# Causal mask of two attentions moved from TensorE to VectorE, with reordered stage heads and earlier row gathers, in a six-stage decoder

## What is computed

```
x += attention(ln(x))            # 16 heads of 32, causal softmax                     "a0"
x += cross(ln(x), ctx, mask)     # softmax over 1024 masked context rows              "m"
x += experts(ln(x))              # 16 routed, 6 per token, sigmoid gate, 2 shared     "f0"
x += grouped_attention(ln(x))    # 32 heads of 64, 8 groups, rms norm, rotary, causal "a1"
x += linear_attention(ln(x), ctx)                                                   # "lin"
x += experts(ln(x))              # 8 routed, 2 per token, 1 shared                    "f1"
```

## Time and profile before

| what | value |
|---|---|
| median of 3 runs | 2163.74 us (2163.08 to 2165.18) |
| the profiled execution itself | 2166.24 us |
| span of its trace | 2165.0 us |
| mean granted TensorE clock in it | 0.941 of full speed |
| busy: TensorE, VectorE, GpSimd, ScalarE | 88%, 52%, 44%, 36% of the span |

### The profile page before, as it was taken

One profiled execution on the slowest core, in us unless ns is written; L12 is line 12 of the kernel. 1 busy time (PEld: TensorE's weight loads), 2 busy tenths in 40 slices (PEclk: granted clock), 3 DMA queues, 4 the chain that ended last, 5 costly groups with the idle time before them and its releaser, 6 DMA issues. The chain is left out here.

```text
span 2165.0 us, 31041 instructions
## 1 busy us (share of the span) xinstructions
PE 1910.6 (88%) x10658; PEld 1625.4 (75%) x10658; DVE 1134.7 (52%) x2385; ACT 780.4 (36%) x2029; POOL 961.7 (44%) x922
## 2 busy tenths in 40 slices
PE   5888978878999999899569999999997899898895
PEld 3776756657899889798447888888876688785784
DVE  4555675446333333235746666666665646456344
ACT  2555543231222222121136555655553323212231
POOL 2332242158872858704636445454442100106584
PEclk7999999999999999899779999999999899799998
DMA  2444432035653546322433233232320210003465
GB/s 83 137 120 124 153 125 78 1 108 199 213 202 119 179 151 219 135 73 88 151 78 98 78 85 103 61 86 77 80 59 26 78 44 1 20 1 101 175 213 172
DMA packets 102630, 232.36 MB, mean 107 GB/s; under 512 B 18752, under 2 KB 19008, under 8 KB 99408
## 3 DMA queue, kind: packets, MB, share of 16 engines
q1 hardware_dynamic: 82736, 144.89, 21.9%
q0 software_dynamic: 19744, 85.47, 11.6%
HBM read 126.23 MB, written 57.93 MB: 85 GB/s over the span
## 5 line engine op out<-in xcount | busy, mean ns | idle before, releaser
L615 POOL TENSOR_SCALAR a_E<-a_E,a_inv 128x128 f32<-128x128 f32 (+3 forms) x384 | 219.3, 589 | 287.4 <-DVE a_inv L734 287.4
L140 PE MATMUL bank<-f_UH,f_XH 128*128 x596 | 203.0, 341 | 19.8 <-POOL f_UL L152 14.8
L729 DVE TENSOR_REDUCE a_top<-bank 128x1 f32<-128x512 f32 (+3 forms) x384 | 164.1, 483 | 83.8 <-PE bank L881 81.3
L649 ACT ACTIVATE a_E<-bank,a_top 128x512 f32<-128x512 f32 (+3 forms) x384 | 199.0, 553 | 9.8 <-DVE a_top L729 9.8
L640 ACT ACTIVATE a_PHL<-bank 128x512 fp32r<-128x512 f32 (+1 forms) x288 | 131.0, 527 | 186.0 <-PE bank L897 185.8
L140 PE MATMUL bank<-f_UH,f_XL 128*128 x596 | 195.3, 328 | 0.0
L140 PE MATMUL bank<-f_UL,f_XH 128*128 x596 | 195.3, 328 | 0.0
L140 PE MATMUL bank<-a_PHL,a_VH 128*128 128x512 f32 (+3 forms) x768 | 181.7, 325 | 0.3 <-DVE a_QL L152 0.3
L152 DVE TENSOR_TENSOR a_PHL<-bank,a_PHL 128x512 fp32r<-128x512 f32 (+1 forms) x288 | 154.4, 590 | 27.3 <-ACT a_PHL L640 26.6
L1569 DVE TENSOR_TENSOR f_gate<-bank,f_gate 128x352 f32<-128x352 f32 x79 | 41.4, 524 | 216.4 <-PE bank L140 216.4
L1515 ACT ACTIVATE f_HH<-bank 128x256 fp32r<-128x256 f32 x220 | 60.0, 325 | 253.5 <-PE bank L1905 253.4
(11 more groups left out here) (384 smaller groups left out, 5130.1 us busy)
## 6 DMA issues: line engine op xcount, KB each, us to landing
f_uraw<-f_up POOLq DMA_DIRECT2D x18, 1408.0 KB, 6.3
f_xb<-table SPq DMA_DIRECT2D x86, 256.0 KB, 2.9
table<-f_ob SPq DMA_DIRECT2D x86, 256.0 KB, 2.1
table<-a_zeros SPq DMA_DIRECT2D x31, 512.0 KB, 4.2
f_draw<-f_down POOLq DMA_DIRECT2D x27, 512.0 KB, 4.2
a_g<-a_f SPq DMA_DIRECT2D x160, 64.0 KB, 2.0
a_raw<-a_qkv SPq DMA_DIRECT2D x36, 256.0 KB, 3.0
f_uraw<-f_up POOLq DMA_DIRECT2D x9, 704.0 KB, 4.8
```

The lines of the kernel that those rows point to most:

```text
L140: m = pe.matmul(out, a, b, start=first and i == 0 and j == 0, stop=last and i == n - 1 and j == 2, skip_group_check=not check)
L615: e.tensor_scalar(self.E[sl][:, a], self.E[sl][:, a], self.inv[:, sl, i:i + 1], 0.0, ALU.mult, ALU.add).then_inc(*self.s_nrm.up(N, m - 1, i))
L649: x = e.activation(self.E[sl][:, self.E_AT[i]:self.E_AT[i] + w], bank[:, off:off + w], ACT.Exp, bias=self.top[:, sl, i:i + 1], accum_out=s ...
L729: e.tensor_reduce(self.top[:, sl, i:i + 1], bank[:, off:off + P * (i + 1)], AX.X, ALU.max, negate=True).then_inc(*self.s_mx.up(N, m, i))
```

## The change

Three edits are made together.

1. *Mask*. The mask matmul goes, and so does the 128 x 128 tile; a 128 x 512 bf16 tile `causal` (zeros, and the triangle in its last 128 columns) is made by GpSimd in each attention. VectorE's maximum becomes one `tensor_tensor_reduce` per row block, which adds mask and scores, negates, writes the result to `E` in SBUF and gives the minimum. ScalarE's exponential reads and writes `E`. The bank is released by VectorE (`s_mx`) and no longer by ScalarE (`s_ex`).
2. *Heads*. m: the first batch's context is loaded by SP in round 20 of a0 and split while the norm's statistics run; on GpSimd the mask work comes after the context's low parts. lin: VectorE begins with the norm; all low parts of the key weights are GpSimd's; the context is loaded right after the key weights and split between norm tiles; its low parts come before those of the value weights. f0, f1: ScalarE's split of the first weights is cut in pieces, each behind a norm tile.
3. *Rows*. The gathers of odd `j` get their own buffers (the idle weight buffers and a few more). Those of `j = 1` are issued as soon as the tiles that can hold such rows are done, ahead of the end of the experts; a gather `j` waits for the add `j-2` and not for `j-1`.

```diff
@@ Attention.pool
+        e.memset(self.causal[:, :], 0.0).then_inc(*self.k.g.up())
         for z in (self.VH, self.VL):
...
+        last = self.causal[:, T - P:T]
+        e.affine_select(out=last, in_=last, compare_op=ALU.is_ge, fill=MASKED, base=0, pattern=[[-1, P]],
+                        channel_multiplier=1).then_inc(*self.s_zero.up(N))
@@ Attention.act
-                        x = e.activation(self.E[sl][:, self.E_AT[i]:self.E_AT[i] + w], bank[:, off:off + w], ACT.Exp,
-                                         bias=self.top[:, sl, i:i + 1], accum_out=self.total[:, sl, i:i + 1])
+                        E = self.E[sl][:, self.E_AT[i]:self.E_AT[i] + P * (i + 1)]
+                        x = e.activation(E, E, ACT.Exp, scale=-1.0, bias=self.top[:, sl, i:i + 1],
+                                         accum_out=self.total[:, sl, i:i + 1])
@@ Attention.dve
+        e.wait_ge(*self.s_zero.after(N))
...
-                        e.tensor_reduce(self.top[:, sl, i:i + 1], bank[:, off:off + P * (i + 1)], AX.X, ALU.max,
-                                        negate=True).then_inc(*self.s_mx.up(N, m, i))
+                        w = P * (i + 1)
+                        e.tensor_tensor_reduce(self.E[sl][:, self.E_AT[i]:self.E_AT[i] + w], self.causal[:, T - w:T],
+                                               bank[:, off:off + w], -1.0, HUGE, ALU.add, ALU.min,
+                                               self.top[:, sl, i:i + 1]).then_inc(*self.s_mx.up(N, m, i))
@@ Attention._pe_scores
-                t = e.matmul(bank[:, off + i * P:off + w], self.k.identb[:, :], self.k.causal[:, :],
-                             start=False, stop=True)
             t.then_inc(*self.s_s.up(N, m, ci))
-            emptied[bk] = self.s_ex.after(N, m, ci)
+            emptied[bk] = self.s_mx.after(N, m, chunk[-1][0])
@@ Attention.sp (a0, round m)
+                if m == 20:
+                    self.k.fetch_context()
@@ Memory.pool
-        self._masks(0)
         self._context_low(e, 0, range(KD), self.s_clo_pool)
+        self._masks(0)
@@ Mixture.pool
-                self._gather_early()
+                self._gather_early(0)
+            if w == W - 1 and self.shared > 1:
+                self._gather_early(1)
         if self.shared == 1:
-            e.wait_ge(*self.s_ev.after(N, "landed", self.OB - 1))
+            self._gather_early(1)
...
-        for j in range(1, self.top):
+        for j in range(2, self.top):
             for i in range(NT):
-                e.wait_ge(*self.s_x.after(N, j - 1, i))
+                e.wait_ge(*self.s_x.after(N, j - 2, i))
                 self._gather(j, i)
@@ Mixture._gather_early(j)
+        if j:
+            e.wait_ge(*self.s_ulo.after(N, W - 1))
+            e.wait_ge(*self.s_dlo.after(N, W - 1))
-        e.reg_load([reg], self.ends[0:1, self.R:self.R + 1])
+        e.reg_load([reg], self.ends[0:1, self.R + j:self.R + j + 1])
         e.wait_ge(self.s_ev.sem, reg)
@@ Mixture.act
-        self.norm.act(self._act_first, lambda i: self._act_logits(0) if i == TT else None)
+        self.norm.act(then=self._act_first)
@@ Mixture._act_first(i), behind norm tile i
+        if i < KD:                  # one of four pieces of UH
+        if i == TT:
+            self._act_logits(0)
+        if KD <= i < KD + 2:        # one of two pieces of DH
@@ Linear.sp
         self._load("k")
+        self._load_context(0, 0)
@@ Linear.pool
+        self._weights_low(e, "k", self.s_wlo_pool)
         for x in "kq":
...
-        self._weights_low(e, "k", self.s_wlo_pool)
@@ Linear.act
-        e.wait_ge(*self.s_fr.after())
-        for x in "kq":
-            e.activation(self.F[x][0][:, :], self.FR[x][:, :], ACT.Copy).then_inc(*self.s_fhi.up(x))
         self._weights_high("k")
-        self.norm.act()
+        self.norm.act(then=self._act_first)   # F behind tiles 0 and 1, the context behind tiles 2 to 5
@@ Linear.dve
-        self._weights_low(e, "k", self.s_wlo_dve)
         self.norm.dve()
+        self._context_low(e, 0, 0, (0, 2), self.s_clo_dve)
```

More of the change, by code:

```diff
@@ L1185, in _pe_scores @@
                     [(self.CH[:, kk, a], self.CL[:, kk, a]) for kk in range(KD)], last=False)
+            if i % TT == 0 and h == 0:
+                e.wait_ge(*self.s_mb.after(b))
             e.matmul(self.k.bank[bk][:, :], self.ones[:, :], self.mb[:, b, a], start=False, stop=True).then_inc(
@@ L1220, in __init__ @@
         self.rows = [sb(f"row{i}", [D])[:, :] for i in range(NT)]
+        raw = self.uraw[:, :, :].rearrange("p k n -> p (k n)")
+        spare = [raw[:, a:a + D] for a in range(0, KD * cols - D + 1, D)] + [self.draw[:, c, :] for c in range(3)]
+        self.back = [self.rows, spare + [sb(f"back{i}", [D])[:, :] for i in range(len(spare), NT)]]
         xb, ob = sb("xb", [self.XB * D]), sb("ob", [self.OB * D])
@@ L1287, in plan @@
         self.s_sent = [sig(f"sent{j}") for j in range(6)]
-        self.s_got = [sig(f"got{i}") for i in range(NT)]
+        self.s_got = [[sig(f"got{x}_{i}") for i in range(NT)] for x in range(2)]
         self.s_passed = sig("passed")
@@ L1315, in plan @@
             self.s_down.plan((N, w), 32)
-        for w in range(self.UB + 1, len(self.experts) + 1):
+        W = len(self.experts)
+        for w in range(self.UB + 1, W + 1):
             self.s_passed.plan((N, w))
-            if w == min(self.R - self.top + 4, len(self.experts)):
-                self.s_passed.plan((N, "early"))
+            if w == min(self.R - self.top + 4, W):
+                self.s_passed.plan((N, "early", 0))
+            if w == (W - 1 if self.shared > 1 else W):
+                self.s_passed.plan((N, "early", 1))
         for j in range(self.top):
@@ L1412, in pool @@
             if w == min(self.R - self.top + 4, W):
-                self._gather_early()
+                for j in range(self.top):
+                    e.wait_ge(*self.s_sent[j].after(N))
+                self._gather_early(0)
+            if w == W - 1 and self.shared > 1:
+                self._gather_early(1)
         if self.shared == 1:
-            e.wait_ge(*self.s_ev.after(N, "landed", self.OB - 1))
+            self._gather_early(1)
         else:
@@ L1624, in _add @@
         e, N, X = self.k.dve, self.name, self.k.X
-        e.wait_ge(*self.s_got[i].after(N, j))
+        e.wait_ge(*self.s_got[j % 2][i].after(N, j))
         e.wait_ge(*self.x_last[i])
-        e.scalar_tensor_tensor(out=X[:, i, :], in0=self.rows[i], scalar=self.wj[:, j, i:i + 1], in1=X[:, i, :],
+        e.scalar_tensor_tensor(out=X[:, i, :], in0=self.back[j % 2][i], scalar=self.wj[:, j, i:i + 1], in1=X[:, i, :],
                                op0=ALU.mult, op1=ALU.add).then_inc(*self.s_x.up(N, j, i))
@@ L1860, in _tables @@
         x = R - self.top
[L1861 removed]
+        e.tensor_scalar(self.ends[0:1, R:R + 2], end[0:1, x:x + 2], float(self.s_ev.value[N, NT - 1] + self.OB), None,
                         ALU.add).then_inc(*self.s_ends.up(N))
@@ L2265, in _weights_high, with _act_first, _context_high @@
             e.activation(self.W[x][0][:, kk, :], self.raw[:, kk, :], ACT.Copy).then_inc(*self.s_whi.up(x, kk))
-    def _context_high(self, b, h):
+    def _act_first(self, i):
+        e = self.k.act
+        if i < 2:
+            x = "kq"[i]
+            e.wait_ge(*self.s_fr.after())
+            e.activation(self.F[x][0][:, :], self.FR[x][:, :], ACT.Copy).then_inc(*self.s_fhi.up(x))
+        elif i < 2 + KD:
+            self._context_high(0, 0, (i - 2,))
+    def _context_high(self, b, h, which):
         e = self.k.act
@@ L2271, in _context_high @@
             e.wait_ge(*self.s_vp.after(b - 1, 4 * h + 3))
-        for kk in range(KD):
+        for kk in which:
             e.activation(self.CH[:, kk, h * 512:h * 512 + 512], self.craw[:, kk, :], ACT.Copy).then_inc(
@@ L2440, in _pe_values_and_features @@
             for d in range(2):
+                if b == 0 and i == 0 and c == 0 and d == 0:
+                    e.wait_ge(*self.s_flo.after("q"))
                 if i % 4 == 0:
@@ L2561, in program @@
         loaded = [s.after() for s in s_in]
+        k.ahead = ExitStack()
+        k.context_ahead(t["ctxT"])
         entry = None
-        for make in (
+        stages = (
                 lambda: Attention(k, "a0", t["a0_qkv"], t["a0_wo"], heads=4, qtiles=1, hd=32),
@@ L2571, in program @@
                 lambda: Mixture(k, "f1", t["f1_up"], t["f1_down"], routed=8, shared=1, gated=False,
-                                router=t["f1_router"], bias=None, top=2)):
+                                router=t["f1_router"], bias=None, top=2))
+        for make in stages:
             stage = make()
@@ L2582, in program @@
             entry = stage.end()
+            if make is stages[1]:
+                k.ahead.close()
         for i in range(NT):
```

99 lines of the change are left out of this document (49 added, 50 removed).

## The result

The changed kernel takes 2131.9 us (median of 4 runs, 2125.4 to 2136.0) against 2164.5 us before; the ratio is 0.984, with an interval of 0.981 to 0.987. The forecast was 2088 us, with a range of 2060 to 2122. The profiled execution took 2136.04 us, that of before 2166.24 us, so 30.2 us have to be found where 75.5 us were expected.

The account below looks back on a forecast made before the run. TensorE was taken to bound a1 (506 of 530 us busy), a0 having slack. 12 + 28 + 5 + 14 - 1 + 12.5 + 5 = 75.5 us off 2166.24, less 2.5 to the median: 2088 us, range 2060 to 2122.

Parts of the forecast that it names:

- Mask on TensorE: Attention loops: dropping four mask matmuls saves 0.40 us a job, 25.6 us in a1 and 6.4 us in a0.
- The waits of a1: a1 loop: extra VectorE work delays low parts, hence the spreading DMAs the scores wait for; 3 us lost.
- The bank in a1: a1 loop: banks come back before ScalarE's exponential, gaining 6 of 7.8 us of TensorE waits.
- The bank in a0: a0 loop: earlier bank release gains a third of 16.2 us of TensorE waits, 5.6 us.
- Mask on VectorE: Attentions: the new maximum takes no longer than the old, 685 ns; bounds 0 and 1.93 us more a job.
- Head of m: Start of m: with the context already there, ScalarE finishes before the first transposed tile; 5 us saved, bounds 3 and 8.5.
- Head of lin: Start of lin: key product starts at about 1684 and not 1697.3 us; 14 us saved, bounds 10 and 16.
- Heads of f0 and f1: First norm tile up to 0.7 us earlier, but pieces delay tiles 5 and 6; 1 us lost for both.
- Rows of f0: End of f0: 32 of 40 gathers remain, eight fewer at 1.56 us each; 12.5 us saved, bounds 10 and 14.
- End of f1: Next eight gathers follow at 2141.3 instead of 2147.3 us; 5 us saved, bounds 1.5 and 6.5.
- the attentions absorb it: Rival, a0 and a1: saved TensorE time returns as waits for spread DMAs and late splits; 40 us lost, 2128; chance 0.19.
- The second pass: Rival, a0 and a1: the new maximum takes 1.93 us more a job on VectorE; 2122 us; chance 0.09.

Follow-up runs that it names:

- the rerun: The changed kernel run once more, unaltered, as reference on another chip: median 2190.3 us, ratio 0.982 to the kernel before.
- the kernels with the low part first: Changed kernel, in a1 VectorE's low part ahead of the maxima, in one also SP's spreads ahead of loads: ratios 0.978 (both orders), 0.976 (VectorE alone).
- the late bank: Changed kernel, but the scores' bank goes back to TensorE only after ScalarE's exponential: ratio 0.981 to the kernel before, a0 290.7 us.
- the turned fill: Changed kernel with one fill of a0 reordered, output products first and the values' transposition last: ratio 0.978 to the kernel before, a0 280.8 us.
- the mask left out: Kernel before with the four mask matmuls of each job deleted and nothing in their place: ratio 0.991 to the kernel before.
- the mask edit alone: Kernel before with only the mask edit, no change to heads or rows: ratio 0.992 to the kernel before, 17.6 us.
- the rest alone: Changed kernel with the mask edit taken back, so heads and rows only: ratio 0.989 to the kernel before, 24.8 us.

## Why the prediction was wrong, step by step

- *Mask on TensorE.* 0.40 us a job was right (1.67 to 1.28 us). The step "25.6 us, all on the path" failed. TensorE's busy time in a1's loop fell by 15.1 us. Some 6 us of the missing 10.5 are clock: 0.97 in this profile, 0.99 in the rerun, which has 484.1 us of work and a loop 7 us shorter (512.3 us). The other 4 us are open.
- *The waits of a1: "I charge 3 us".* This step failed most. The waits for the spread grew by 11.6 us. The chain of maxima, low part, spread and scores is as long as before while TensorE's round is shorter; the kernels with the low part first showed it, 10 to 20 us.
- *The bank in a1: 6 us.* The waits for the exponential did go, all 7.8 us of them. But the late bank brings them back (8.0 us) and leaves a1 at 584.1 us, with 13.4 us of waits for the spread where the early bank has 18 to 20. So the term is nothing while the spread comes late. Together: 15.1 us of work, 7.8 us of these waits, less 11.6 us, less 1 us of small ones, is the 10 us measured.
- *The bank in a0: "I take a third".* The step named the right bank and the right late engine, and then still gave the change 5.6 us for it, and 6.4 us for the masks. 0.6 us came. What was missing: an earlier start in front of a fixed release makes one longer stand out of two short ones, and behind it the clock fell in two rounds of four. The late bank and the turned fill show it.
- *Mask on VectorE.* Right that the instruction takes what the old one took; the accumulator read was missed. What both cost is bounded by the mask left out: 2 us in a1 against the mask edit alone, 4.6 us against the late bank.
- *Head of m.* 3.2 us against 5, inside its bounds (3.8 us between the experiments' means). The mechanism was right: four centrings beside the low parts were to be done at 318.6 us, and were at 318.3.
- *Head of lin.* The key product starts 13.1 us earlier (forecast 14). The stage gained 8.0. Behind the product, the same instructions take 261.4 us at a clock of 0.91 before, 266.5 at 0.89 after. But both experiments with the old lin have 266.4 and 266.9 us at 0.89 as well, and two with the new lin have 262.2 and 262.5 us at 0.91. So these 5 us are scatter of the clock between executions and not the edit. Among the experiments the new stage is 13 to 18 us shorter than the old: that is in keeping with the forecast of 14.
- *Heads of f0 and f1: "1 us for both".* 1.1 and 3.3 us. The pieces in front of late norm tiles cost what was charged, 0.9 us in f1. What was put at nothing is the clock: with the new order it fell in the router product in five kernels of eight, with the old in none of six.
- *Rows of f0: 8 x 1.56 us.* Eight gathers went, but the others became longer, 1.79 us each: the adds of `j = 0` and `j = 1` now run one after the other just when the gathers of `j = 2` are issued. 5.9 us of 12.5 came, and 1.8 us by an earlier start.
- *End of f1.* From the last tile's copy to the end 3.9 us less (forecast 5); the head took them back.

Of the rivals, "the attentions absorb it" came true for 29 of its 40 us; it had 0.19. That its full price, 2128 us, is so near to the measured 2131.9 is luck: the other 16 us were lost in m, f0, lin and f1. It deserved more: its eight waits and the late split stood in the earlier trace rows. The second pass and the lock-out did not happen.

## What to carry to other kernels

When work is taken from an engine that is busy 95% of the time, look for the chain that runs from its own output over the others back to its next input, and compare its length with the new round; what is shorter than that chain is waited away, until a link is moved up. Freeing a resource earlier helps only if the next one needed is free as well; otherwise, as in a0, the stand is only moved and joined. Price a gather on GpSimd together with what VectorE does beside it. Before a few microseconds of a stage are put down to an edit, look at the granted clock and at the same stage in kernels that leave it alone: here that took 5 us out of lin and over 2 us out of f1's head.

## What the runs showed of the hardware

TensorE's clock fell to 1.2 GHz behind one stand of 1.95 us, and stayed at 2.4 GHz behind stands of 1.05 and 0.41 us in the same round. Of four stands of 1.9 us in the changed kernel's a0 two were followed by a fall.

GpSimd's issue of an indirect DMA takes 0.95 us alone and up to 4.7 us beside VectorE's adds of two float32 operands in SBUF; the long ones end 0.8 us after the run of adds. The Trainium skill (SBUF — State Buffer, "SBUF: two separate sides") describes this stall of the descriptors for VectorE's two-port mode, and a lock by two SBUF inputs only against a GpSimd operation that reads SBUF. Here adds with two SBUF inputs hold up the issue, which reads its indices from SBUF.

On the three chips of the experiments TensorE stands still in f0 for 36 to 49 us, in one or two stands, and VectorE with it; on the first chip its longest stand there is 8 us. Two stretches of the kernel with the rest alone, in which GpSimd issues its row stores (columns as in the earlier trace rows):

```profile
522.30:537.30 15.00, 0.00 (x0) 0.00 (x0) 0.00 (x0) 0.46 (x1) 11.35 (x13) 0.50 0.65 234
537.30:552.30 15.00, 0.00 (x0) 0.00 (x0) 0.00 (x0) 0.00 (x0) 11.34 (x13) 0.50 0.55 211
```

The trace names no releaser for it, and the first chip does not have it, with the same instructions. What it is stays open.
